# An attention layer with post-norm: twelve probability slots, two query slots reloaded by halves, keys once per batch, two accumulating transfers, one ones product per half

## The reference

```python
qkv = x @ Wqkv                                   # 32 query heads of 32, one key, one value
scores = einsum('bqhd,bkd->bhqk', q, k) * d**-0.5
scores = where(pos_k <= pos_q, scores + slope[h] * (pos_k - pos_q), -1e30)
probs = softmax(scores)
attn = einsum('bhqk,bkd->bqhd', probs, v).reshape(B, S, H)
x = layernorm(x + attn @ Wo)
w = fake-quantized weight (int4, groups of 128)
x = layernorm(x + x @ w.T + bias)
```

## Time and profile before

| | |
|---|---|
| three runs | 2259.36, 2260.26, 2260.34 us; median 2260.26 |
| profiled execution | 2261.66 us, of which the span from first to last instruction is 2259.9 us |
| busy: PE, DVE, ACT, POOL | 2214.5 (98%), 1662.0 (74%), 999.0 (44%), 919.4 (41%) us |
| granted PE clock | 0.996 of full speed over the span |
| stages | `project` to about 462 us, `attend` to about 1520 us, `finish` to the end |
| DMA | 257.02 MB, mean 114 GB/s; queue q1 holds the 16 engines 38.8% of the span |

### The profile page before, as it was taken

The page is one execution under the profiler, slowest core; times in us unless marked ns, Lnnn a source line. Parts: engine busy times, 40 slices in busy tenths (PEclk is TensorE's granted clock), DMA queues, the critical chain, the costliest instruction groups (busy, mean ns, idle before and its releaser), DMA issues.

```text
span 2259.9 us, 36072 instructions
## 1 busy us (share of the span) xinstructions
PE 2214.5 (98%) x12303; PEld 1517.2 (67%) x12303; DVE 1662.0 (74%) x5002; ACT 999.0 (44%) x1950; POOL 919.4 (41%) x559
## 2 busy tenths in 40 slices
PE   7999999999999999999999999989999999999998
PEld 6888888655555555555555555537888888888887
DVE  6977778878888888888888888845656565656554
ACT  4222222167777777777777777770101010101010
POOL 0000000058878888887888887760101010101010
PEclk9999999999999999999999999999999999999999
DMA  6555554653442443343233223256333333333220
GB/s 232 190 182 194 202 186 141 178 126 89 110 100 77 114 110 82 95 114 99 56 95 91 73 76 96 58 174 179 91 95 91 93 92 91 94 89 97 87 80 28
DMA packets 179837, 257.02 MB, mean 114 GB/s; under 512 B 15446, under 2 KB 105686, under 8 KB 179306
## 3 DMA queue, kind: packets, MB, share of 16 engines
q1 hardware_dynamic: 179510, 254.87, 38.8%
q10 hardware_dynamic: 180, 0.33, 0.0%
HBM read 166.89 MB, written 87.20 MB: 112 GB/s over the span
## 4 chain that ended last, share of the span: by engine, by line
PE 70%; ACT 4%; DVE 3%; POOL 1%; issue 1%; SPq 1%; DMA 1%; ACTq 0%; POOLq 0%; DVEq 0%
PE pf L1418 30%; PE pa L1155 12%; PE pa L242 11%; PE pa L1139 11%; PE pa L1179 5%; ACT probs L1244 4%; DVE xm L261 2%; PE pf L1443 1%; POOL probs L1110 1%; DMA xk<-recip_d 1%; SPq L1317 0%; PE pa L251 0%; POOL probs L1096 0%; DVE late L1284 0%; DVE yt_lo L1563 0%
## 5 line engine op out<-in xcount | busy, mean ns | idle before, releaser
L1244 ACT ACTIVATE probs<-pa,slope 128x512 f32<-128x512 f32 (+3 forms) x1536 | 773.0, 588 | 241.6 <-PE pa L1139 147.2
L261 DVE CUSTOM_DVE_ANT_0 xm<-pa,xm 128x128 bf16<-128x128 f32 (+1 forms) x1488 | 750.3, 554 | 133.2 <-PE pa L242 120.5
L1110 POOL TENSOR_TENSOR probs<-probs 128x1024 f32<-128x1024 f32 x252 | 686.9, 2726 | 105.3 <-PE pa L1155 84.6
L1515 POOL TENSOR_TENSOR yb<-y,xm 128x1024 f32<-128x1024 f32 x32 | 76.6, 2395 | 648.1 <-DVE z L1528 632.7
L1155 PE MATMUL pa<-probs,v 128*32 128x512 f32 (+3 forms) x3072 | 307.1, 495 | 2.9 <-POOL probs L1096 2.9
L1472 ACT ACTIVATE ln<-ln 128x1 f32<-128x1 f32 x64 | 13.0, 203 | 490.2 <-DVE ln L1548 490.2
L1096 POOL TENSOR_SCALAR_AFFINE_SELECT probs<-probs 128x512 f32<-128x512 f32 x256 | 159.3, 634 | 107.1 <-ACT probs L1244 107.1
L1418 PE MATMUL pf<-ff_lo,xk 128*128 128x512 f32 x512 | 199.7, 390 | 0.0
L1089 POOL MEMSET credit<- 128x1 f32 x4 | 0.2, 98 | 460.8 <-POOLq L350 460.8
L681 ACT ACTIVATE q_hi<-ps,qscale 128x512 fp32r<-128x512 f32 x64 | 43.9, 688 | 283.8 <-PE ps L568 265.4
L1418 PE MATMUL pf<-fo_hi,xk 128*128 128x512 f32 x512 | 164.7, 393 | 0.0
(11 more groups left out here) (159 smaller groups left out, 4267.1 us busy)
## 6 DMA issues: line engine op xcount, KB each, us to landing
xm<-in_L_attn_hidden_states SPq DMA_DIRECT2D x8, 2048.0 KB, 9.3
q_hi_d<-q_hi SPq DMA_DIRECT2D x64, 256.0 KB, 2.0
q_lo_d<-q_lo SPq DMA_DIRECT2D x64, 256.0 KB, 2.4
att_d<-att SPq DMA_DIRECT2D x64, 256.0 KB
xm<-in_L_attn_hidden_states SPq DMA_DIRECT2D x32, 512.0 KB, 3.8
out<-z SPq DMA_DIRECT2D x32, 512.0 KB, 2.6
q<-q_hi_d SPq DMA_DIRECT2D x62, 256.0 KB, 6.0
xq<-q_hi_d SPq DMA_DIRECT2D x44, 256.0 KB, 5.2
```

Source lines behind the costliest of these rows:

```text
L261: nc.vector.tensor_tensor_reduce(out=unused[:, 0:keys], in0=bank[:, 0:keys], in1=sh.distance[:, d0:d0 + keys], scale=1.0, scalar=-3e38, op ...
L1110: nc.gpsimd.tensor_tensor(o, o, probs[:, source % PR, h0:h1, 0:N], ALU.add).then_inc(add_done, 1)
L1244: nc.scalar.activation(probs[:, n % PR, h, 0:N], sc_ps[sc_ring.bank[use]][:, at:at + N], ACT.Exp, scale=slope[:, bass.ds(g * HPG + h, 1)]) ...
L1515: nc.gpsimd.tensor_tensor(yb[:, :], y[:, u, :], bias[:, :], ALU.add).then_inc(yb_done, 1)
```

## The change

- `probs` gets twelve slots: six as before (`KEPT`) and six in `more_probs`, which lies where `fo_lo` and `q2` lie later (`MORE`). Unit n takes the slot that unit n of the previous iteration had, save in the last iteration, which uses the six kept slots only.
- Queries have two slots and are reloaded by halves: half 0 of t + 2 when half 0's scores of t are done, half 1 when all scores of t are done (`load_half`). Keys and values are loaded once per batch (`load_keys`, `load_values`), instead of once per iteration.
- Two additions are done by DMAs that POOL issues with `accum_op=ALU.add` (`send`): 6 into 7 and 4 into 5, 1 MB each. POOL then adds 5, 7 and 9 into 8 (with 11 into 10 and 10 into 9 before), and 3 into 2 and 2 into 1. One ones product per half is left, of units 0 and 8; those of units 4 and 9 are gone.
- `fo_lo` can no longer be loaded early: its eight parts are loaded in the last iteration, when the slots over it have been read, and `half_of_third` follows it.
- The copies of attended values move from DVE to ACT (the last one excepted), at fixed places between exponentials (`ACT_STEADY`). `add_second` moves to a place just ahead of the last three row maxima (`ADD_SECOND_AT = 47`).
- The 128 + 512 keys of the maxima of query block 4 are cut into 320 + 320.
- The order on PE is one list for the whole iteration (`STEADY`), with scores and maxima interleaved finely, and another for the last iteration (`LAST`).

```diff
-SLOTS = 3
+SLOTS = 2
+KEPT, MORE = 6, 6
+HALVED = (BPH + 1) * P // 2
+PIECES += [(1, h, qb, k0, HALVED if qb == BPH else min((qb + 1) * P - k0, CH))
+           for h in range(HPG) for qb in range(BPH, QB) for k0 in (0, HALVED if qb == BPH else CH)]
...
+        fo = [ctx.enter_context(nc.sbuf_tensor("fo_hi", [P, KT, H], f32r))]
+        with ExitStack() as before_weights:
+            more_probs = before_weights.enter_context(nc.sbuf_tensor("more_probs", [P, MORE, HPG, CH], fp32))
+        fo.append(ctx.enter_context(nc.sbuf_tensor("fo_lo", [P, KT, H], f32r)))
...
+    STEADY = (
+        "O0- V8- S M+ M+ M+ S S M+ V10- M+ M+ S M+ L S S M+ V9- M+ M+ S M+ S M+ M+ S S M+ S M+ M+ V6- V11- M+ "
+        "S M+ M+ S S M+ M+ S M+ S M+ S M+ S M+ V0 M+ M+ S M+ S S M+ M+ S M+ V2 V1 V3 M+ S S M+ S M+ M+ S T+ "
+        "V4 M+ M+ S M+ S S M+ M+ S M+ O8- V5 M+ M+ S S M+ M+ S V7 S S M+ M+ M+ S S S"
+    ).split()
+    POOL_STEADY = [
+        (1, ("send", 6, 7)), (1, ("cut", 9)), (1, ("cut", 11)), (1, ("add", 11, 10)), (0, ("cut", 0)),
+        (1, ("add", 5, 8)), (1, ("add", 10, 9)), (0, ("cut", 2)), (0, ("cut", 3)), (0, ("cut", 1)),
+        (1, ("add", 7, 8)), (1, ("add", 9, 8)), (0, ("add", 3, 2)), (0, ("add", 2, 1)), (0, ("cut", 8)),
+        (0, ("send", 4, 5)), (0, ("cut", 10)),
     ]
+    ACT_STEADY = [(16, "attended", 1, 1), (27, "attended", 0, 0), (37, "sums", 1, 1), (48, "sums", 0, 0)]
+    ADD_SECOND_AT = 47
+
+    LAST = ("O0- S S L V8- V10- S S V9- S S S S V6- V11- O8- O7- S S S O5- O9- V0 V1 S S S S V2 V3 S S S S V4 O0 V5 S S S S "
+            "S S S S V6 O4 S S S S V7 S S S S V8 S S O7 S O8 V9 V10 O9 V11 O10 O11").split()
...
+    def slot(t, n):
+
+        return (t * NU + n) % (KEPT + MORE) if t < ITS - 1 else ((ITS - 1) * NU % (KEPT + MORE) + n) % KEPT
...
+                if not last and not before_last:
+                    sp.wait_ge(sc_done, t * SC + scores_of[BPH])
+                    load_half(sp, sh, q3[u], q_hi_d, q_lo_d, t + 2, 0)
...
+                if t % NG == 2 and t // NG < B - 1:
                     sp.wait_ge(pv_done, block_done["V", NU - 1, t - 1])
+                    load_keys(sp, t // NG + 1)
+                    load_values(sp, t // NG + 1)
...
                 if last:
+                    sp.wait_ge(sc_done, (ITS - 1) * SC)
                     first_tiles(sp)
+                if not last:
+                    put_max(sp, sh, q3[(u + 1) % SLOTS], t + 1, 0, mx_use[t + 1, ("turn", 0)] + 1)
                 if not first:
                     put_att(sp, t - 1, 1)
...
                 if last:
+                    for s in range(KEPT, KEPT + BPH):
+                        unit_read(sp, *tenant[s])
+                        for k in (2 * (s - KEPT), 2 * (s - KEPT) + 1):
+                            sp.dma_start(raw(seam.fo[1][:, k:k + 1, :]), wo_d[1, :, k:k + 1, :]).then_inc(seam.w3_in[1], 16)
+                    for s in range(KEPT + BPH, KEPT + MORE):
+                        unit_read(sp, *tenant[s])
                     half_of_third(sp)
+                if not last and not before_last:
+                    sp.wait_ge(sc_done, (t + 1) * SC)
+                    load_half(sp, sh, q3[u], q_hi_d, q_lo_d, t + 2, 1)
                 put_att(sp, t, 0)
...
+            def send(source, to, t):
+
+                may_add("send", source, to, t)
+                assert span(units[source])[1] == span(units[to])[1] == CH
+                pool.dma_start(prob(t, to), prob(t, source), accum_op=ALU.add).then_inc(sent_added[source, to], 16)
```

More of the change, by code:

```diff
@@ L518, in _ @@
             every_step(NCH, 2, body)
-            sp.wait_ge(sh.loaded[1], FIRST_HALF)
+            sp.wait_ge(sh.half_in[1][0], HALF_IN)
             for n in range(2):
@@ L944, in late_in_last @@
-    def late_in_last(x):
-        return x[2] == ITS - 1 and x[0] == "O" and x[1] > 6
-    tail = [(x[0], int(x[1:]), ITS - 1) for x in TAIL]
-    block_list = [x for t in range(ITS) for n in range(NU) for x in blocks_of(t, n) if not late_in_last(x)] + tail
+    STEADY = (
[3 rows of a table added]
+    ).split()
[4 more added lines that the diff above has]
+        (0, ("send", 4, 5)), (0, ("cut", 10)),
+    ]
@@ new lines, in attend, with sequence, left_out @@
+    ACT_LAST = [(16, "attended", 1, 1), (18, "sums", 1, 1), (22, "attended", 0, 0), (28, "sums", 0, 0)]
+    def sequence(t):
+        return [(x[0], int(x[1:].rstrip("+-")) if x[0] in "VO" else None, t + x.count("+") - x.count("-")) for x in (LAST if t == ITS - 1 else STEADY)]
+    def pool_steps(t):
+        found = [(*step, t - back) for back, step in (POOL_LAST if t == ITS - 1 else POOL_STEADY) if t - back >= 0]
+        return [x for x in found if not left_out(x)]
+    def left_out(x):
+        return x[0] != "cut" and x[-1] >= ITS - 2 and x[2] == BPH * HALF
@@ L954, in attend @@
-    for t, x in add_list:
-        read_by_add[t, x[1]] = add_count[t, x]
-        added_to[t, x[2]] = add_count[t, x]
+    SENT = sorted({x[1:3] for t in range(ITS) for x in pool_steps(t) if x[0] == "send"})
+    readers, writers = {}, {}
+    for t in range(ITS):
+        for x in pool_steps(t):
+            if x[0] != "cut":
+                readers.setdefault((x[3], x[1]), []).append(x)
+                writers.setdefault((x[3], x[2]), []).append(x)
     EXPS = HPG * NU
@@ L1188, in block_product @@
                     total(t, n)
+            scores_order = [(n, j) for n in range(NU) for j in range(HPG // heads_at_once(units[n]))]
             def body(t, u, i):
[L1191 to L1211 removed]
@@ new lines, in body @@
+                to_score, to_max = iter(scores_order), iter(maxima[t])
+                for kind, n, s in sequence(t):
+                    if kind == "S":
+                        n, j = next(to_score)
+                        if j == 0 and n in (0, BPH):
+                            pe.wait_ge(neg_max[u][n // BPH], (i + 1) * PUTS)
+                        scores(t, u, n, j)
+                    elif kind == "V" and s >= 0:
+                        values(s, n)
+                    elif kind == "O" and s >= 0:
+                        total(s, n)
+                    elif kind in "MTL":
+                        found = next(to_max)
+                        if not found:
+                            continue
+                        w, item = found
+                        if item == ("piece", 0):
+                            pe.wait_ge(sh.keys_in[w // NG % 2], 16 * (w // NG // 2 + 1))
+                            pe.wait_ge(sh.half_in[w % SLOTS][0], (w // SLOTS + 1) * HALF_IN)
+                        if item == ("piece", BPH * HPG):
+                            pe.wait_ge(sh.half_in[w % SLOTS][1], (w // SLOTS + 1) * HALF_IN)
+                        maxima_item(w, w % SLOTS, item)
@@ L1213, in tensor @@
             every_step(ITS, SLOTS, body)
-            for product in tail:
-                block_product(*product)
         def scalar(act):
```

273 lines of the change are left out of this document (128 added, 145 removed), and 12 rows, old and new, of the table plan.

## The result

The changed kernel takes 2456.17 us (median; 2453.09 to 2459.16) against 2260.04 (2259.36 to 2260.34): a ratio of 1.087, 95% interval 1.085 to 1.089. It is slower by 196 us, where 2193 was forecast and 2245 was the upper end.

What follows compares the result with a forecast made beforehand. PE's work with 5% coupling loss was taken as the bound before, POOL's closed chain after. The stage summed to 30 x 30.7 + 28.9 + 37.5 + 3 = 990.4 us against 1057.5, giving 2193 us, range 2150 to 2245.

Steps and rivals of the forecast that it cites:

- the paragraph on half loads: Query reloads by halves in the attention stage: cover 3.9 us for queries, 1.2 for turned maxima, both priced at nothing.
- the transfer is late: Rival: addition 5 to 8 waits for send 4 to 5, delaying POOL's chain; 2305 us at X = 11; slower, chance 0.11.
- X: Time from issue to landing of send 4 to 5; taken as 7.4 us, ends 5.2 and 8.6, 1 more if meeting loads.
- POOL's chain: Closed loop from cut 0 through POOL's additions, DVE's sum and O0- back to cut 0: 30.7 us, setting the period.
- PE's own price: PE's work per steady iteration, counted from distances between starts: 31.2 us before the change, 29.3 after.
- coupling loss: About 1.7 us, 5%, of every period before the change in which PE was taken to stand waiting.
- The ones products: Those of units 4 (1.00) and 9 (0.76) go: 1.76 us of PE work a period, on the bound.
- S: What issuing one transfer costs POOL, twice a period: taken as 1.0 us, between 0.45 and 2.4.
- The first iteration: First iteration of the attention stage: the period less 1.8 us, 28.9 us.
- The last iteration: Last iteration of the attention stage, PE with about 31 us of work: 37.5 us, ends 35 and 41.
- That copy: Attended copy waiting in ACT's queue behind value product 11 or 3; PE needs the bank 3 us after; priced at nothing.
- The seam: Behind the attention stage: output weight's low part loaded later but hidden, later loads slip; 3 us lost, ends 0 and 12.

Runs made afterwards that it cites:

- small sends: Changed kernel with both accumulating transfers left in place but carrying 64 KB instead of 1 MB each: 2205.2 us, 0.975 of before.
- both simple moves, later and earlier: Changed kernel with 6 into 7 issued behind addition 5 to 8: 2359.2 us; changed kernel with both transfers issued earlier: 2339.5 us.

## Why the prediction was wrong

**The step that failed** is the paragraph on half loads: cover of 3.9 us for the queries and 1.2 for the turned maxima, "Both at nothing". Its landing times of 5.9 and 1.8 are those of the earlier trace rows, taken from a queue without sends. The rows for the right sum were there. By the earlier trace rows the DMA engines had 0.38 x 32.9 = 12.5 us of work in a period of before. The same prediction priced each send at 3.4 us of transfer at its low end and twice that at its high end, and it put the half load "in the same microsecond" as the send. It then charged the meeting to the send alone, 1 us, and nothing to the load. On the engines, both pay: 2 x 5.5 us of sends stand in the window of loads that have 3.9 and 1.2 of cover. What was measured: landings of 13.8 and 9.4, a stall of 6.1, and 2.0 more by the clock, a term which the forecast did not have at all. The cover itself was read rightly: from the first issue of the half load to piece 16 it is 10.2 us (922.67 to 932.85) with small sends, where issue and landing take 6.1, so some 4 are left. In the changed kernel the rows are in 16.2 us after the first issue (920.24 to 936.49), 6.0 too late. 31 x 8.1 = 251 us, which is the difference to the kernel with small sends.

**The rival "the transfer is late"** had the right resource and the wrong victim. It priced lateness by X on POOL's chain, where X = 9.1 would cost 1.7 us a period; the wait there is 0.9, and PE's query load is hit first. Its chance of 0.11 followed from the argument that the DMA queues "have much room in this stage", a mean where the burst decides. (X stands for send 4 to 5: 9.1 measured, where the estimate from the Trainium skill's pages "DMA: Bandwidth & Descriptors" and "Collectives: The Full Stack" was 12.3. Send 6 to 7 took 13.5. The 2345 of that estimate was also reached through POOL's chain, which was not what bound.)

**PE's own price** was mis-sized: 29.3 forecast, 30.7 measured. Counting products by distances gave 31.2 for the kernel before and left 1.7 of "coupling loss". But PE was busy for 198.8 of 200 us, and the trace says where the 1.7 goes. The prices of scores and maxima were read among their like; beside a value or ones product they are dearer. In the run with small sends:

```profile
925.16 0.63 PE L1200 MATMUL pa<-xk 116*128 116x512 f32 x2
925.63 0.40 PE L245 MATMUL pa<-xk,xq 96*128 96x512 f32 x1
925.96 0.64 PE L1213 MATMUL pa<-more_probs,v 128*32 128x256 f32 x8
```

The two scores take 0.235 each, the maximum product of the same width, right ahead of a value product, 0.33. Added up from start to start over 700 to 1300 us, scores and maxima take 19.8 us a period, where the forecast had 18.0, and value products, ones products and transposes 10.9 (11.3): 30.7. Of the scores and maxima 1.9 us are what those beside the nine blocks of value and ones products take above the price among their like. For the kernel before the same sum gives 20.1 and 12.8, that is 32.9, its whole period; some 0.6 of it are single products up to 0.3 us over their price, which may be waits.

**POOL's chain** was overpriced by as much. In the same run it goes from cut 0 to the end of addition 2 to 1, and on to the sum on DVE:

```profile
928.05 0.63 POOL L1144 TENSOR_SCALAR_AFFINE_SELECT probs<-probs 128x512 f32<-128x512 f32 x1
...
947.59 2.38 POOL L1163 TENSOR_TENSOR probs<-probs 128x1024 f32<-128x1024 f32 x1 [0.23 <-POOL probs L1163]
951.25 1.75 DVE L1331 TENSOR_TENSOR probs<-probs 128x1536 f32<-128x1536 f32 x1
```

From 928.05 to 949.97 it is 21.9 us, where the sum had 23.3: the ten gaps of 0.17 are 0.8 us in all, and the additions 18.8 instead of 19.1. From O0- (922.57) to cut 0 it is 5.5, as forecast. With the 1.9 of the sum on DVE the chain is 29.3 long, under PE's 30.7, and most of the difference shows as 1.3 us between the end of POOL's addition and the start of DVE's, which stands in DVE's own queue behind row maxima. So the forecast's period came out right by two errors that cancelled: PE dearer by 1.4, and POOL's chain cheaper by 1.4. That the kernel with small sends has the period of the forecast is luck.

**The ones products** (1.76, on the bound; 3.6 us a period before and 1.8 after by the sum of starts) and **S** (0.87 for 1.0) were right. **The first iteration** was too (28.8 for 28.9), but partly by luck: with small sends it takes 26.9.

**The last iteration**: 37.5 forecast (35 to 41); 55.2 measured. Without large sends it is still 48.5. In that stretch of the kernel with small sends:

```profile
1418.00:1466.50 48.50, 40.30 (x273) 13.63 (x272) 10.68 (x11) 29.16 (x62) 25.60 (x19) 0.89 0.78 260
```

PE is busy for 40.3 us where I had counted 31. The mean clock of 0.89 means some 10.7 us at half clock, which makes about 5 us of that difference (an estimate from this row). PE stands for 8 more: 2.0 at the first ones product of its own units, which waits for DVE and so for POOL, and 1.2 and 0.65 at value products whose bank waits for an attended copy on ACT (`<-ACT att L1285`). That copy was priced at nothing, and in this iteration the cover fails. In the changed kernel the larger part of the further 6.7 is one wait of PE for send 6 to 7, 3.8 us ahead of O7-.

**The seam** was forecast at 3 lost; the rest of the kernel after the attention stage took 2.9 us less than before. The load of the output weight's low part was hidden, as the step had it, and the slip behind it did not show: DVE's wait for tile 2's reciprocals, 5.5 us in the earlier trace rows, is 4.0. Probably it was covered by the stage's later end, as its transfers stand in the last iteration; no run separates this. With small sends the rest behind the stage is also 736.6 us (2203.1 - 1466.5).

**Sum for the kernel without the DMA effect.** On the profiled execution 2194.6 was forecast, and with small sends it took 2205.2. The 11 us are the last iteration (11 more than forecast), the steady ones (by the starts of O0-, 30.9 instead of 30.7, 7 us) and a stage that begins 1 us later, less 6 at the seam and 2 in the first.

**Open.** Whether sends issued in smaller pieces, spread over the period, would keep both the loads and slot 6 on time. It was not tried: both simple moves, later and earlier, ran into another wait. Nor was the other remedy, an earlier place for the half loads or more work of PE ahead of piece 16.

## What to carry to other kernels

Where a change adds transfers, sum the engine time of everything issued within the cover of the nearest deadline, not the mean share of the stage, and price each existing load again in that queue: here 11 us of added engine time turned loads of 5.9 and 1.8 us into 13.8 and 9.4. Removing the wait that the profile names shows only the next customer of the same resource; shrink the resource's load instead, as the run with small sends did, and the whole cost shows at once. And when the profile says that an engine is busy for 99% of a stage, try the sum in which that is simply true before you invent a loss to explain the rest.

## What the runs showed of the hardware

- An accumulating transfer of 1 MB within SBUF held all 16 DMA engines for 5.5 us in the changed kernel (5.1 to 5.9 in the other runs), a plain one for 3.2. Issuing it took 0.87 us of POOL's time at 64 KB as at 1 MB, and 0.57 without the addition. In company it landed in 7.1 to 13.5 us, at 64 KB in 2.8 to 4.3.
- A load of 8 KB that lands in 1.8 us in a quiet queue took up to 9.4 behind large transfers that another queue had issued: small size did not protect it. The issue of two query loads on SP, 0.91 us in the earlier trace rows, took 1.84 in the full stretch; but that is not by the sends alone, for a single load's issue took 1.91 in the kernel without sends.
- Some 6 us of standing in every 39 cost 2.0 us more by the granted clock, and filler products during the stand gave that back.
- A score or maximum product of 512 columns took 0.235 us among its like and 0.33 beside a value or ones product, which here is 32 columns wide for each head. Nine blocks of these in a period of 30.7 us cost PE 1.9 us in this way.
